# Expert results weighted per slot and added to the residual rows by accumulating scatters, instead of gathered back per token

## The reference

```
xf = layernorm(x)                       # x: input + graph part + attention part
logits = xf @ Wg + bg                   # 8 experts
top_w, top_i = top_k(logits, 2); top_w = softmax(top_w)
for e in range(8):
    h = gelu(xf @ W1[e] + b1[e])        # 256 -> 1024
    out += w_dense[:, e:e+1] * (h @ W2[e] + b2[e])
x = x + out
```

## Time and profile before

| what | us |
|---|---|
| median of 3 runs | 3043.88 (3043.86 to 3047.2) |
| profiled execution, its own time | 3049.32 |
| span of its trace | 3047.6 |
| gate and placing, from the stage's start to the first expert matmul | 2456 to 2546.8 |
| 29 expert tiles | 2546.8 to 2975.9 |
| from the last expert matmul to the end | 71.7 |

### The profile page before, as it was taken

The page is one execution under the profiler, slowest core; times in us unless marked ns, Lnnn a source line. Parts: engine busy times, 40 slices in busy tenths (PEclk is TensorE's granted clock), DMA queues, the critical chain, the costliest instruction groups (busy, mean ns, idle before and its releaser), DMA issues. The chain is left out here.

```text
span 3047.6 us, 39832 instructions
## 1 busy us (share of the span) xinstructions
PE 2602.3 (85%) x13041; PEld 1681.5 (55%) x13041; DVE 1592.3 (52%) x3093; ACT 651.8 (21%) x1191; POOL 1291.3 (42%) x1342
## 2 busy tenths in 40 slices
PE   1589899968999999889999997988988948999990
PEld 1343445536555555665555566555444647888880
DVE  4469887725555554465655544667777742000003
ACT  0321100031111112411111133122212312333320
POOL 0000000027777772377777705777777001111126
PEclk6699899989999999899999998999999957999995
DMA  1330076544454552544555425444444160222113
GB/s 50 104 106 1 1 266 231 203 138 133 140 157 145 157 157 83 155 144 133 152 159 156 148 90 158 133 130 141 140 139 134 34 197 24 64 92 90 62 50 115
DMA packets 211512, 374.19 MB, mean 123 GB/s; under 512 B 28898, under 2 KB 163459, under 8 KB 211206
## 3 DMA queue, kind: packets, MB, share of 16 engines
q1 hardware_dynamic: 149318, 203.45, 20.4%
q0 software_dynamic: 62016, 168.51, 19.3%
HBM read 299.54 MB, written 72.31 MB: 122 GB/s over the span
## 5 line engine op out<-in xcount | busy, mean ns | idle before, releaser
L1415 POOL DMA_INDIRECT g_ring<-h_rows,idx x780 | 771.6, 989 | 237.8 <-issue 207.0
L1086 PEld LDWEIGHTS g_pagg<-g_onehot,g_ring 128*128 128x128 f16 x4704 | 324.9, 98 | 404.7 <-issue 267.5
L1086 PE MATMUL g_pagg<-g_onehot,g_ring 128*128 128x144 f16 x4704 | 393.8, 228 | 139.7 <-DMA g_ring<-h_rows,idx 89.8
L1415 POOL DMA_INDIRECT g_ring<-xn_rows,idx x390 | 383.1, 982 | 118.9 <-issue 105.8
L1257 DVE TENSOR_TENSOR g_agg<-g_agg,g_pagg 128x288 f32 x585 | 265.7, 454 | 250.7 <-PE g_pagg L1086 207.8
L1260 DVE SCALAR_TENSOR_TENSOR g_onehot<-iota_keys,shift,keys 128x288 f16<-128x288 f16 x585 | 299.4, 513 | 1.0 <-DVE g_pre_at L1249 1.0
L1889 DVE TENSOR_TENSOR f_ys<-f_bank,f_b 128x256 f32<-128x256 f32 x58 | 24.6, 425 | 411.6 <-PE f_bank L1841 411.6
L1349 DVE SCALAR_TENSOR_TENSOR g_t<-g_ph,g_bh,g_rT 128x448 f32<-128x448 f32 (+1 forms) x144 | 90.0, 625 | 267.6 <-PE g_ph L1163 253.5
L1163 PE MATMUL g_pi<-g_agg,g_wc 128*128 128x448 f32 (+1 forms) x576 | 226.6, 517 | 0.0
L1163 PE MATMUL g_pr<-g_hT,g_wh 128*128 128x448 f32 (+1 forms) x576 | 223.9, 512 | 0.0
L1163 PE MATMUL g_pr<-g_agg,g_wc 128*128 128x448 f32 (+1 forms) x576 | 220.6, 506 | 0.0
(11 more groups left out here) (345 smaller groups left out, 3465.5 us busy)
## 6 DMA issues: line engine op xcount, KB each, us to landing
ma_R<-q_cols SPq DMA_DIRECT2D x27, 896.0 KB, 9.8
f_w<-in_L_ffn_W SPq DMA_DIRECT2D x16, 1024.0 KB, 7.5
h_cols<-g_hn SPq DMA_DIRECT2D x36, 448.0 KB, 4.4
h_rows<-g_rows SPq DMA_DIRECT2D x36, 448.0 KB, 3.5
g_hT<-h_cols SPq DMA_DIRECT2D x36, 448.0 KB, 5.9
mix_R<-q_cols SPq DMA_DIRECT2D x15, 896.0 KB, 10.0
g_ring<-h_rows,idx POOLq DMA_INDIRECT x780
ma_R<-q_cols SPq DMA_DIRECT2D x9, 1120.0 KB, 5.6
```

Of the source, the lines that this page charges most:

```text
L1086: mm = e.matmul(pg[:, k * TYPES:(k + 1) * TYPES, :].rearrange("p t d -> p (t d)"), ring[:, slab, c, o:o + P], hot[:, c, :], start=(c == 0 ...
L1415: e.indirect_dma_start(ring[:, b % SLABS, c, :], None, tables[s], bass.IndirectOffsetOnAxis(ap=idx[:, o:o + 1], axis=0)).then_inc(landed[b ...
```

## The change

The weights are made before the placing. The one-hot product gets 128 columns instead of 64: 64 give a row number, 64 the slot's weight (`slot_weight`). Row numbers are made so that an empty slot of lane p points at row 3136 + p, one of 128 spare rows that `acc_rows` has grown (`SPARE`); `src` is the same clamped to 3135, for the gathers of inputs. DVE adds the bias and multiplies by the slot's weight. POOL no longer runs a loop of gathers alone: its loop issues the two gathers of tile t+2, and then two indirect DMAs with `compute_op=ALU.add` that add the two halves of tile t to rows of `acc_rows`; after each it waits until it has landed. At the end one DMA copies `acc_rows` to `out`, from HBM to HBM. `slots_out`, `acc`, the return gathers, the weighting passes, 15 of the 16 stores of zeros and the load of `acc` are gone.

```diff
         def dve_choose(e, step):
-            step(e.tensor_copy(ids[:, :], id_i[:, :]))
+            step(e.tensor_scalar(ids[:, :], id_i[:, :], -float(SPARE), None, ALU.add))
 ...
         def dve_lanes(e):
             for j in range(4):
-                e.tensor_tensor(lane[j % 2], ... is_equal)
-                e.tensor_tensor(b[:, :, :], ... is_equal)
-                e.wait_ge(S["lane"], 3 * j + 2)
-                e.tensor_tensor(b[:, :, :], b[:, :, :], ids[...], ALU.mult)
+                e.tensor_tensor(block_of[:, :, :], ... is_equal)
+                e.tensor_tensor(lane[j % 2], ... is_equal)
+                e.wait_ge(S["lane"], 4 * j + 2)
+                e.tensor_tensor(b[:, :, 0:BLOCKS], block_of[:, :, :], row_less[...], ALU.mult)
+                e.tensor_tensor(b[:, :, BLOCKS:], block_of[:, :, :], weight[...], ALU.mult)
+                e.wait_ge(S["lane"], 4 * j + 4)
 ...
             @block.sync
-                for k in range(USED, SLOTS // P):
-                    e.dma_start(slots_out[k * P:(k + 1) * P, :], none[:, :])
+                e.dma_start(acc_rows[SPARE:SPARE + P, :], none[:, :])
                 load(1)
-                e.dma_start(acc[:, :, :], acc_rows...)
-                for x in range(XPT):
-                    ...
-                    with expert_tiles(e, x) as t:
-                        for c in range(2):
-                            e.wait_ge(S["result"], t * 2 + c + 1 + 2)
-                            e.dma_start(slots_out[bass.ds(t * ST + c * P, P), :], ys[:, c, :])
-                for a, b in PARTS:
-                    ...
+                total = e.value_load(first_tile[0:1, XPT:XPT + 1], ...)
+                for x in range(1, XPT - 1):
+                    before_x = e.value_load(first_tile[0:1, x:x + 1], ...)
+                    e.wait_ge(S["expert_sum"], before_x * 2 + 2)
+                    load(x + 1)
+                e.wait_ge(S["added"], total * 2 + 2)
+                e.dma_start(out[:, :], acc_rows[0:N, :]).then_inc(S["stored"], 16)
 ...
             @block.gpsimd
-                with e.Fori(0, end) as t:
-                    e.wait_ge(S["xturned"], t + 1)
-                    e.tensor_copy(now[:, :], idx[:, bass.ds(t * 2, 2)])
-                    ...
-                    for c in range(2):
-                        e.indirect_dma_start(xg[:, c, :], None, xf, ...)
-                (28 gathers into rows, 28 into y)
+                fetch(src[:, 0:2])
+                e.wait_ge(S["xturned"], 2)
+                fetch(src[:, 2:4])
+                with e.Fori(0, total) as t:
+                    e.wait_ge(S["xturned"], t + 3)
+                    e.tensor_copy(now[:, :], src[:, bass.ds(t * 2 + 4, 2)]).then_inc(S["now"], 1)
+                    e.wait_ge(S["now"], t + 1)
+                    fetch(now)
+                    e.tensor_copy(past[:, :], idx[:, bass.ds(t * 2, 2)]).then_inc(S["past"], 1)
+                    e.wait_ge(S["past"], t + 1)
+                    for c in range(2):
+                        e.wait_ge(S["result"], t * 2 + c + 1 + 2)
+                        e.indirect_dma_start(acc_rows, bass.IndirectOffsetOnAxis(ap=past[:, c:c + 1], axis=0), ys[:, c, :], None, compute_op=ALU.add).then_inc(x_st[c], 16)
+                        e.wait_ge(x_st[c], t * 16 + 16)
+                        e.sem_inc(S["added"], 1)
 ...
             @block.vector
                 dve_choose(e, step)
+                dve_weights(e, step)
                 dve_place(e, step)
+                step(e.tensor_tensor(row_less[:, :, :], ids[...], part[:, 0, :, :], ALU.subtract))
                 dve_lanes(e)
-                e.tensor_copy(idx[:, 0:SLOTS // P], pidx)
-                dve_weights(e, step)
+                step(e.tensor_copy(lane_f[:, :], lane_i[:, :]))
+                step(e.tensor_scalar(idx[:, 0:SLOTS // P], found[:, 0:SLOTS // P], lane_f[:, 0:1], None, ALU.add))
+                e.tensor_scalar(src[:, 0:SLOTS // P], idx[:, 0:SLOTS // P], NP - 1, None, ALU.min)
+                step(e.tensor_copy(slot_weight[:, :], found[:, SLOTS // P:]))
                 ...
                             e.wait_ge(S["expert_sum"], t * 2 + c + 1 + 2)
-                            e.wait_ge(x_st[c], t * 16 + 16)
-                            e.tensor_tensor(ys[:, c, :], p2[c], b2[:, x, :], ALU.add)
-                (56 multiply-adds into acc)
+                            e.wait_ge(S["added"], t * 2 + c + 1)
+                            e.tensor_tensor(ys[:, c, :], p2[c], b2[:, x, :], ALU.add)
+                            e.tensor_tensor(ys[:, c, :], ys[:, c, :], slot_weight[:, bass.ds(t * 2 + c, 1)]..., ALU.mult)
```

More of the change, by code:

```diff
@@ L144, in gps_layer_kernel @@
     gnn(nc, A, tables, [hT0] + hTs, idx0, idx1, keys, bases, main_at, shift, tab, iota_keys, ident, acc_rows, xf)
-    with nc.sbuf_tensor("acc", [PT, TILES, C], F32) as acc:
-        ffn(nc, A, acc, acc_rows, ident, ones, xf, slots_out, out)
+    ffn(nc, A, acc_rows, ident, ones, xf, out)
 def edge_tables(nc, A, ones, keys, bases, main_at, shift, idx0, idx1, tab):
@@ L1562, in _, with ffn @@
                             dve_moments(e, v, step)
-def ffn(nc, A, acc, acc_rows, ident, ones, xf, slots_out, out):
+def ffn(nc, A, acc_rows, ident, ones, xf, out):
     with ExitStack() as ctx:
@@ L1591, in ffn @@
         part_i, part = sb("part_i", [PT, 2, 2, TILES], I32), sb("part", [PT, 2, 2, TILES])
-        idx, now = sb("idx", [P, SLOTS // P + 2], I32), sb("now", [P, 2], I32)
+        idx, now, past = sb("idx", [P, SLOTS // P + 4], I32), sb("now", [P, 2], I32), sb("past", [P, 2], I32)
+        src = sb("src", [P, SLOTS // P + 4], I32)
+        lane_i, lane_f = sb("lane_i", [P, 1], I32), sb("lane_f", [P, 1])
+        row_less = sb("row_less", [PT, 2, TILES])
+        slot_weight = sb("slot_weight", [P, SLOTS // P])
         xg = sb("xg", [P, 2, C])
@@ L1611, in ffn @@
         px = bank[6][:, :].rearrange("p (k n) -> p k n", k=KC)
-        S = {n: sem(f"f_{n}") for n in ("dve", "acc_in", "turned", "copied", "logits", "set", "made", "gate_in", "zeroed",
+        S = {n: sem(f"f_{n}") for n in ("dve", "turned", "copied", "logits", "set", "made", "gate_in", "zeroed",
                                         "gap", "exp", "taken", "counts", "offsets", "ranks", "placed", "lane", "found", "idx", "bias",
-                                        "now", "xturned", "xcopied", "hidden_sum", "hidden", "expert_sum", "result", "expert_done", "weights", "used", "stored", "paced")}
+                                        "now", "xturned", "xcopied", "hidden_sum", "hidden", "expert_sum", "result", "plain", "past", "added", "stored", "paced")}
         x_in = [sem(f"f_expert_in{i}") for i in range(2)]
@@ L1617, in ffn @@
         x_st = [sem(f"f_expert_stored{i}") for i in range(2)]
[L1618 to L1619 removed]
+        fetched = nc.alloc_semaphore("f_fetched")
         NFT = SLOTS // ST
[L1621 removed]
         def expert_tiles(e, x):
@@ L1769, in _ @@
                                 base=0, pattern=[[1, PT]], channel_multiplier=-1).then_inc(S["made"], 1)
-                e.memset(idx[:, :], 0).then_inc(S["made"], 1)
+                e.iota(lane_i[:, :], [[1, 1]], base=SPARE, channel_multiplier=1).then_inc(S["made"], 1)
+                e.memset(src[:, :], 0).then_inc(S["made"], 1)
+                e.wait_ge(S["zeroed"], 16)
                 e.wait_ge(S["idx"], 1)
-                end = e.value_load(first_tile[0:1, XPT + 1:XPT + 2], min_val=2, max_val=NFT + 1)
@@ L1819, in _ @@
                 for j in range(4):
-                    e.wait_ge(S["lane"], 3 * j + 3)
+                    e.wait_ge(S["lane"], 4 * j + 4)
                     for i in range(HALF):
-                        mm = e.matmul(pidx, lane[j % 2][:, i, :], tile_id[j % 2][:, i, :], start=(j == 0 and i == 0), stop=(j == 3 and i == HALF - 1))
+                        mm = e.matmul(found, lane[j % 2][:, i, :], row_and_weight[j % 2][:, i, :], start=(j == 0 and i == 0), stop=(j == 3 and i == HALF - 1))
                     mm.then_inc(S["found"], 1)
@@ L1875, in _ @@
                 dve_choose(e, step)
+                dve_weights(e, step)
                 dve_place(e, step)
+                step(e.tensor_tensor(row_less[:, :, :], ids[:, :].unsqueeze(1).to_broadcast([PT, 2, TILES]), part[:, 0, :, :], ALU.subtract))
                 dve_lanes(e)
                 e.wait_ge(S["found"], 4)
-                e.tensor_copy(idx[:, 0:SLOTS // P], pidx).then_inc(S["idx"], 1)
-                dve_weights(e, step)
+                e.wait_ge(S["made"], 7)
+                step(e.tensor_copy(lane_f[:, :], lane_i[:, :]))
+                step(e.tensor_scalar(idx[:, 0:SLOTS // P], found[:, 0:SLOTS // P], lane_f[:, 0:1], None, ALU.add))
+                e.tensor_scalar(src[:, 0:SLOTS // P], idx[:, 0:SLOTS // P], NP - 1, None, ALU.min).then_inc(S["idx"], 1)
+                step(e.tensor_copy(slot_weight[:, :], found[:, SLOTS // P:]))
                 e.wait_ge(S["bias"], 32)
-                for c in range(2):
```

(7 more changed lines are left out.)

60 lines of the change are left out of this document (19 added, 41 removed).

## The result

The changed kernel takes 2998.1 us, median of 4 runs (2994.17 to 2998.73), against 3043.87 before (4 runs, 3040.11 to 3047.2); the ratio is 0.9844, with a 95% interval of 0.983 to 0.9857. The profiled execution took 2997.88, its span is 2996.2. The forecast was 2995, in a range of 2984 to 3030.

What follows compares the result with a forecast made beforehand. PE was taken to bound the experts, and POOL's return gathers most of the 71.7 us end. From 3049.32, -51.2 at the end and +2.1 in the placing gave 3000.2; less 5.4 for the median, 2995, range 2984 to 3030.

Steps and rivals of the forecast that it cites:

- The end: Behind the last expert matmul: 71.7 us of gathers, weighting and stores become 20.5, a gain of 51.2 us.
- from the data to the scatter's issue: At the end: 0.3 us to reach the last scatter plus 0.65 us delay by the first half's scatter.
- scatter: At the end: the last accumulating scatter lands in 3.7 us, the middle of 2.8 and 4.5.
- copy and its issue: At the end: HBM-to-HBM copy of 3.2 MB, 14 us between 10 and 18.5, plus 0.6 for semaphore and issue.
- The placing: Ahead of the experts: added weights, lane products and index steps, less POOL's saving, cost +2.1 us, between 0 and +4.
- +0.9: In the placing: PE's 128-column product costs 8 ns more for each of 112 matmuls, the weight load setting the pace.
- 5.1 + 2s: Experts: POOL's cycle per tile, s being a scatter's landing; 12.5 us at 3.7, hidden under PE's 14.71 up to 4.8.
- still waits for PE once per tile: Experts: expected profile sign that POOL's cycle stays hidden under PE; if gone, POOL has become the bound.
- Rivals 1 and 2: Experts: POOL becomes the bound, mildly at landings of 4.8 to 5.65 us (chance 0.13), or making the kernel slower (0.12).
- rival 2: Experts: scatter landings above 5.65 us make the kernel slower; at 6.5, +98 us, 3093; chance 0.12.
- Rival 3: At the end: the copy to `out` runs at a quarter of the best rate, +22 us, 3017; chance 0.09.
- Rival 4: In the placing: the wider product doubles, load and product one after the other, +25 us, 3019; chance 0.04.

Runs made afterwards that it cites:

- e_narrow: Changed kernel with PE multiplying only the 64 row-number columns and a constant 0.5 as the slots' weights; 3003.78 us.
- e_late: Changed kernel with POOL waiting for each tile's second scatter only behind the next tile's gathers; 2992.53 us.
- e_third: Changed kernel with one more accumulating scatter, of zeros, issued and waited for after each tile's first scatter; 3123.12 us.
- e_plain: Changed kernel with scatters that write without adding, so the residual is left out of the result; 2988.93 us.
- e_early_pair: e_early with both halves' scatters in flight together, POOL waiting for both behind the next tile's gathers; 2980.81 us.
- e_nocopy: Changed kernel with only the first 128 rows copied to the output at the end; 2985.6 us.
- e_early: Changed kernel with the residual rows copied to the output beside the gate and the scatters adding into the output itself; 2991.24 us.

## Why the prediction was right, and where it was off

- **The end.** Forecast -51.2, measured 20.2 - 71.7 = -51.5. Its terms: bias and multiply 1.2, measured 1.11 (2976.00 to 2977.11); from the data to the scatter's issue 0.3 + 0.65 = 0.95, measured 2.07; scatter 3.7, measured 3.95 up to the copy's issue; copy and its issue 14.6, measured 13.07. The second is a step that I mis-sized: I took 0.3 us from one scatter's landing to the next one's issue, where the trace has 0.9 (landed at 2978.28, issued at 2979.18), and a scatter that waits for no other starts 0.8 behind its data (2973.67 to 2974.49). The copy was mis-sized the other way: it landed in 12.0 us, not 14, and the 1.07 behind its landing had no term. The errors, +1.4 and -1.6, cancel, which is luck: the whole is right to 0.3 us. The 9.3 us that the prediction worked out from the fit of the Trainium skill ("DMA: Bandwidth & Descriptors", section Anatomy of one DMA) are 2.7 short of the 12.0; the page gives the fit for DMAs that GpSimd issues, and this one is SP's.
- **The placing.** Forecast +2.1, measured -2.5 (51.4 for 53.9). All terms but PE's summed to +1.2; e_narrow, where PE's product is as before, shows +1.6. The term that failed is the product: "+0.9" by the weight load's pace at 1.2 GHz, measured -4.1. The width raised the granted clock, and the product took 20.1 us for 24.2. I had named the case ("If the wider product raised the granted clock in this stretch, it would be less") but given it no number and no chance.
- **The experts.** Forecast 0, measured +0.3. The cycle was forecast as 5.1 + 2s, 12.5 at s = 3.7; it is 13.6 with s = 3.9, as the gap behind the first scatter's landing is 0.9 and that behind the second's 0.5, where I counted 0.3 for each; the rest is small (gathers and their gaps 3.34 for 3.20, the second index copy with its gaps 1.09 for 1.3). The edge is then not at s = 4.8 but near 4.4. So the sign "still waits for PE once per tile" held in 16 of 29 tiles only. That s is above its mean beside the loads of weights came as forecast. That a late POOL costs nothing is shown by e_late, which takes the lateness away and gains nothing in the tiles.
- **Rivals 1 and 2** did not come, by 1.1 us per tile. e_third shows that the mechanism is real and as dear as rival 2 said: one wait of 4.7 us more turns -46 into +79 us.
- **Rival 3**: the copy landed in 12.0 us, not 36, at 320 GB/s behind its fixed part. **Rival 4**: product and weight load overlap at 128 columns, at either clock (4.80 and 4.80 us busy within 4.80 at 0.50, 3.39 and 3.20 within 3.43 at 1.00).
- **The median.** Profile against profile the forecast was -49.1 and the spans differ by 51.4; the medians differ by 45.8. I carried the 5.4 us that the profiled execution of before lay above its median over to after, where profile and median agree (2997.88 and 2998.1). So such a gap does not come with every profile. I take them for the spread of the unchanged part, whose end moves by 12 us between the traces; that is not shown, since the unprofiled runs have no trace.

## What to carry to other kernels

Where results return to rows in HBM, accumulate them as they are made: the return then lies beside PE as long as the issuing engine's cycle fits under PE's, and only the last piece's landing is left at the end. Write out the issuing engine's cycle with its own landings in it, and compare it with the bound engine's period at the landing times beside other traffic, since each wait for a landing there is dear once the cycle is longer; put the wait behind the engine's next work, or don't wait between pieces with different rows. If the rows that are added to must be copied anyway, copy them first, where nobody waits for DMA, and add into the output.

## What the runs showed of the hardware

- An accumulating scatter of 128 rows of 1 KB lands in 3.8 to 3.9 us (median), a plain one in 2.4 (e_plain); POOL writes descriptors for 1.6 us instead of 0.97.
- Beside a load of 2 MB of weights it takes longer: the next instruction of POOL stands up to 2.0 us later (6.78 for 4.65 to 4.81 behind the first scatter, 6.47 for 4.36 to 4.47 behind the second); one tile without a load showed 5.68 behind the first.
- From one scatter's landing to the next one's issue on POOL, with a semaphore wait between, are 0.9 us (2978.28 to 2979.18); between two DMAs without a wait, 0.30.
- A scatter whose rows are all beyond the bound (rows from 3136, bound 3124, in e_early_pair) still lands, in 2.7 us:

```profile
out<-f_none,f_lane_i POOLq DMA_INDIRECT x2, 2.7
```

- A copy of 3.2 MB from HBM to HBM, in 64 pieces of 50 KB, lands in 12.0 us, one of 128 KB in 2.5 (e_nocopy); beside loads of weights the large one takes 19.5 (e_early).
- Gapless matmuls of 64 columns did not raise TensorE's clock from 1.2 GHz in 24 us (before and e_narrow); those of 128 columns did after 3.8 to 6.1 us (eight traces), and it fell again behind 1.9 to 2.2 us in which PE was idle. The wider product was faster in absolute time, 20.1 us for 24.2.
